# Expert rows loaded as 32 by 32 blocks and transposed by VectorE, in place of a TensorE transpose

## The chip, the cores and the metric

The kernel runs on one core of one Trainium2 chip. The metric is the device time of one execution in microseconds (us). The kernel before took 1431.74 us (median of 3 runs, 1426.88 to 1431.79).

## What is computed

Four blocks follow each other, each with a residual sum and a layer norm: an attention with 16 heads over 16 batches of 256 rows, a mixture of experts, a second attention with 16 heads of width 8, and a gated recurrence. The change touches the second block only. Cut to it:

```python
def _L0_ffn_ref(x, keys, w1, b1, w2, b2, rw, rb):      # E, TOP_K = 16, 4;  D = 128;  F = 512
    logits = -dist2 + jnp.einsum('bld,ed->ble', x, rw) + rb
    topv, topi = jax.lax.top_k(logits, TOP_K)
    w = jax.nn.softmax(topv, axis=-1)
    hidden = jax.nn.gelu(jnp.einsum('bld,efd->blef', x, w1) + b1, approximate=False)
    exp_out = jnp.einsum('blef,edf->bled', hidden, w2) + b2
    sel = jnp.take_along_axis(exp_out, topi[..., None], axis=2)
    return jnp.sum(w[..., None] * sel, axis=2)
```

Each of the 4096 rows goes to 4 of 16 experts.

## The kernel before, in words

**Stages.** The first stage computes the first attention and the router, and GpSimd scatters each row of 128 floats four times into the DRAM tensor `xs`, sorted by expert. The expert stage (about 689 to 977 us of the profiled span) then works through `xs` in NT = 144 tiles of GT = 128 rows. The second attention and the recurrence follow; their loops end the kernel. Every engine has a program of its own, written out by hand in this order, and semaphores join them.

**The expert stage, tile n.**
- SyncE (SP) reads the tile's row number out of the SBUF tensor `plan` (`row_of`, L416), loads the 128 rows (64 KB) from `xs` into `xg`, a ring of four buffers (`load_rows`, L423; the first four at L462), and later stores the tile's result from `yrow` into the same rows of `xs` (`store_rows`, L429). Its loop (L463 to L474) issues the load of tile n + 4, then the store of tile n - 4. It also carries the first transfers of the second attention (L439, L446, L454, L456) between tiles 95 and 102. SP executes in order: whatever it spends on one issue delays all that follow.
- TensorE (PE) transposes the rows with a multiplication by `ident` into a PSUM bank (`rows_in`, L899), two tiles ahead; it multiplies with the first weights (L911, four matmuls, each shown as two in the trace) and, for tile n - 2, with the second (L922, the same number).
- VectorE (DVE) copies the weights of tile n + 2 out of `wall` (L1473 and L1476), copies the transposed rows from PSUM to `xgT` (`rows_T`, L1480) and adds the bias to the result of tile n - 2 (L1502).
- ScalarE (ACT) applies the Gelu to the four hidden blocks (L1175).
- GpSimd (POOL) gathers finished rows for the second attention (L598), paced by the semaphore of `wA`.

`xg`'s buffer n % 4 is free for tile n + 4 when tile n has been transposed: `load_rows` waits for `tin_mm`, which PE raises.

The one place in which the order of SP's work is written:

```python
            for n in range(NT + 4):
                if n + 4 < NT:
                    load_rows(n + 4)
                if n >= 4:
                    store_rows(n - 4)
```

Of the kernel before, what the change touches and what calls it, by code (L numbers as in the profile page):

```python
# [12 lines left out]
B, N, D = 16, 256, 128  # L13
# [14 lines left out]
BIG = 1.0e30  # L28
EPS = 1e-5
GT = 128  # L30
CAP = TOK + GT
DUMMY = E * CAP
NT = (TOK * TOPK + E * (GT - 1)) // GT
NT += NT % 2
FULL = TOK * TOPK // GT
ROWS = DUMMY + (NT - FULL) * GT
LEVELS = TOK // GT
WA = F + FC
# [74 lines left out]
def build(nc, t, out):  # L113
    ctx = ExitStack()
    with ctx:
        def sb(name, shape, dt=fp32, c=ctx):
            return c.enter_context(nc.sbuf_tensor(name, shape, dt))

        def sem(name):
            return ctx.enter_context(nc.semaphore(name))  # L120

        psum = ctx.enter_context(nc.psum_tensor("psum", [128, 8 * 512], fp32))
        bank = [psum[:, i * 512:(i + 1) * 512] for i in range(8)]


        ident = sb("ident", [128, 128])
# [29 lines left out]
        a = ExitStack()  # L156
# [103 lines left out]
        xg = sb("xg", [128, 4, D], c=e2)  # L260
        xgT = sb("xgT", [128, 4, GT], c=e2)
        wA = sb("wA", [128, 4, WA], c=e2)
# [18 lines left out]
        tg = sb("tg", [128, N])  # L281


        TI, DN = [bank[3], bank[4]], [bank[5], bank[6]]
        S0, S1, PTA, PTB, OTB, J, Y, M = bank

        def up(n, f):

            return bank[(2 * n + f // 2) % 3][:, (f % 2) * GT:(f % 2 + 1) * GT]

        def rows_of(b):
# [3 lines left out]
        xs = nc.dram_tensor("xs", (ROWS, D), fp32, kind="Internal").ap()  # L295
# [6 lines left out]
            scores shifted_ready exps rinv_ready pn_ready pn1_ready pt_mm ptA_ev ptB_ev pv_mm ot_ev wo_mm res_ready bo_mm  # L302
            var_ready pow_ready x1c_ready m_x x1T_ready m_l mask_ready m_r pos_ready xsq_ready x1_kept scat exp_w top_ready
            ksq_ready rmat_ready b2_kept a_done plan_ready zrow_ready plan_out plan_in filled
            b2_mm xg_in0 xg_in1 xg_in2 xg_in3 tin_mm xgT_ready wA_ready wB_ready up_mm hid_ready dn_mm yrow_ready ys_out0 ys_out1
            cw_in lora_mm c_set cleared mrow_in to_full to_free st_full exps1 s_full max_done pv_full o_free full0 full1 free0 free1 a1_ready parts_ready
            qkd_out stk zeros_out nm_ready x2_ready x2_kept x3_ready x3_kept gate_act scan_done
            yk_in0 yk_in1 gates_in weighed comb_done var2_ready pow2_ready posc_ready xo_kept h_full fin_dve var3_ready pow3_ready scale_ready h_act fin_ready out_done""".split()
        s = {n: sem(n) for n in names}
# [11 lines left out]
        def need(eng, name, n):  # L321

            if not isinstance(n, int) or n > 0:
                eng.wait_ge(s[name], n)

        def need_alone(eng, name, n):


            if not isinstance(n, int) or n > 0:
                eng.wait_ge(s[name], n)  # L330
                eng.sem_inc(s["went_on"], 1)
# [42 lines left out]
        def _(sp):  # L374
# [17 lines left out]
            nothing = zrow[:, :].rearrange("q (o d) -> q o d", o=1).to_broadcast([128, E, D])  # L392
            for c in range(CAP // 128):
                if c % 2 == 0 and c > 0:
# [15 lines left out]
            sp.wait_ge(s["plan_in"], 16)  # L410
            sp.wait_ge(s["filled"], 16 * (CAP // 128 + 1))

            def row_of(n):
                at = 2 * n + 1
                src = plan[0:1, at:at + 1] if isinstance(n, int) else plan[0:1, bass.ds(at, 1)]
                return sp.value_load(src, min_val=0, max_val=ROWS - GT)  # L416

            row = {}

            def load_rows(n):  # L420
                need_alone(sp, "tin_mm", n - 3)
                row[n] = row_of(n)
                sp.dma_start(xg[:, n % 4, :], xs[bass.ds(row[n], GT), :]).then_inc(s[f"xg_in{n % 4}"], 16)  # L423

            def store_rows(n):

# [32 lines left out]
                row[n] = row_of(n)  # L459
            sp.wait_ge(s["scat"], 16 * B * TT * TOPK)  # L460
            for n in range(4):
                sp.dma_start(xg[:, n, :], xs[bass.ds(row[n], GT), :]).then_inc(s[f"xg_in{n}"], 16)  # L462
            for n in range(NT + 4):  # L463
                if n + 4 < NT:
                    load_rows(n + 4)
                if n >= 4:
                    store_rows(n - 4)
                if n == 95:
                    store_parts(-2)
                if n == 98:  # L470
                    sp.wait_ge(s["zeros_out"], 16)
                    sp.wait_ge(s["cleared"], 1)
                if n in (98, 100, 102):
                    load_stack(-2, 0, (n - 98) // 2)  # L474
# [24 lines left out]
        def _(pool):  # L499
# [4 lines left out]
            for it in range(TT):  # L504
# [8 lines left out]
                   allow_small_or_imprecise_dtypes=True).then_inc(s["cst"], 1)  # L513
            g.iota(first_row[:, :], pattern=[[CAP // 16, E]], base=0, channel_multiplier=0,
                   allow_small_or_imprecise_dtypes=True).then_inc(s["cst"], 1)
# [219 lines left out]
        def _(pe):  # L735
# [156 lines left out]
            pe.wait_ge(s["b2_kept"], E // 4)  # L892


            def rows_in(n, buf, loads):

                need(pe, f"xg_in{buf}", loads)
                need(pe, "xgT_ready", n - 1)
                nc.tensor.transpose(TI[buf % 2][:, 0:GT], xg[:, buf, :], ident[:, :]).then_inc(s["tin_mm"], 1)  # L899

            rows_in(0, 0, 16)
            pe.wait_ge(s["c_set"], 1)
            def tile(n):
                if n < NT:
                    need(pe, "xgT_ready", n + 1)
                    need(pe, "wA_ready", n + 1)
                    need(pe, "hid_ready", 4 * n - 4)
                    for f in range(FC):
                        if f == 2:
                            need(pe, "hid_ready", 4 * n - 2)  # L910
                        mm(up(n, f), wA[:, n % 4, f * 128:(f + 1) * 128], xgT[:, n % 4, :], start=True, stop=True).then_inc(s["up_mm"], 1)  # L911
                if n == 0:
                    rows_in(1, 1, 16)
                if n + 2 < NT:
                    rows_in(n + 2, (n + 2) % 4, 16 * ((n + 2) // 4 + 1))
                if 0 <= n - 2 < NT:
                    m = (n - 2) % 4
                    need(pe, "hid_ready", 4 * n - 4)
                    need(pe, "wB_ready", n - 1)
                    need(pe, "yrow_ready", n - 3)  # L920
                    for f in range(FC):
                        last = mm(DN[n % 2][:, 0:D], hid[:, m, f, :], wB[:, m, f * D:(f + 1) * D], start=(f == 0), stop=(f == FC - 1))  # L922
                    last.then_inc(s["dn_mm"], 1)
# [157 lines left out]
            for n in range(NT + 2):  # L1081
                tile(n)
                if n == 82:
                    attention(-3, -3 % 3, (7,))
                if n == 86:
                    attention(-2, -2 % 3, (1,))
                if n == 116:
                    attention(-2, -2 % 3, (7,))
# [190 lines left out]
        def _(dve):  # L1279
            v = nc.vector  # L1280
# [160 lines left out]
            v.tensor_scalar(used[:, :], tile_e[:, :], float(E), None, ALU.is_lt)  # L1441
            v.scalar_tensor_tensor(tile_r[:, :], tile_e[:, :], float(CAP), tile_r[:, :], ALU.mult, ALU.add)
            v.tensor_scalar(plan2[:, :, 0], tile_e[:, :], float(E - 1), None, ALU.min)
# [24 lines left out]
            def expert_of(n):  # L1468
                src = plan[0:1, 2 * n:2 * n + 1] if isinstance(n, int) else plan[0:1, bass.ds(2 * n, 1)]
                return dve.value_load(src, min_val=0, max_val=E - 1)  # L1470

            def weights_A(e, par):
                v.tensor_copy(wA[:, par, :], wall[:, bass.ds(e, 1), 0:WA].rearrange("q o c -> q (o c)")).then_inc(s["wA_ready"], 1)  # L1473

            def weights_B(e, par):
                v.tensor_copy(wB[:, par, :], wall[:, bass.ds(e, 1), WA:WCOLS].rearrange("q o c -> q (o c)")).then_inc(s["wB_ready"], 1)  # L1476

            def rows_T(n, buf):
                need(dve, "tin_mm", n + 1)
                v.tensor_copy(xgT[:, buf, :], TI[buf % 2][:, 0:GT]).then_inc(s["xgT_ready"], 1)  # L1480

            for n in range(2):
                first = expert_of(n)
                weights_A(first, n)
                weights_B(first, n)
            for n in range(2):
                rows_T(n, n)

            def tile(n):
                q = (n + 2) % 4  # L1490
                if n + 2 < NT:
                    e = expert_of(n + 2)
                    need(dve, "hid_ready", 4 * n - 4)
                    weights_A(e, q)
                    need(dve, "up_mm", 4 * n - 4)
                    rows_T(n + 2, q)
                if 0 <= n - 2 < NT:
                    m = (n - 2) % 4
                    need(dve, "dn_mm", n - 1)
                    if n >= 6:  # L1500
                        need(dve, f"ys_out{n % 2}", 16 * ((n - 6) // 2 + 1))
                    v.tensor_tensor(yrow[:, m, :], DN[n % 2][:, 0:D], wB[:, m, FC * D:FC * D + D], ALU.add).then_inc(s["yrow_ready"], 1)  # L1502
                if n + 2 < NT:
                    need(dve, "yrow_ready", n - 1)
                    weights_B(e, q)
# [204 lines left out]
```

## Time and profile before

| | |
|---|---|
| median of 3 runs | 1431.74 us |
| lowest and highest | 1426.88 and 1431.79 us |
| span of the profiled execution | 1445.1 us |
| mean granted TensorE clock over it | 0.960 of full speed |
| busy: PE, PE weight loads, DVE, ACT, POOL | 88%, 67%, 70%, 64%, 53% |

The profiled execution's record starts with its first and ends with its last instruction; no time around this span is listed for it, and the span is 13.4 us above the median of the runs. "Busy" counts instructions that compute. SP's instructions (register operations and the issue of transfers) are never counted as busy, so SP has no share on the page: its load is read from the timeline of its own queue, written SPq. A matmul here is a float32 one and appears as two instructions.

### The profile page before, as it was taken

The numbers are of one execution on the slowest core, as the hardware profiler recorded it, in microseconds if no ns is written. First come the engines' busy times: TensorE is split into PE (matmuls) and PEld (weight loads), VectorE is DVE, ScalarE is ACT, GpSimd is POOL, SyncE is SP. The second block draws the span as 40 slices with busy tenths as digits, with TensorE's granted clock in tenths as the row PEclk, the third lists the DMA queues.
The fourth block names the chain that finished last, engine by engine and source line by source line (L and its number), as shares of the span: only waits on it lengthen the run. The fifth ranks groups of instructions, "written<-read, shape, count | busy, mean of one in ns | idle before, by whom it ended". The sixth has DMA issues, their size and how long they took to land.

```text
span 1445.1 us, 36685 instructions
## 1 busy us (share of the span) xinstructions
PE 1272.4 (88%) x9756; PEld 971.6 (67%) x9756; DVE 1014.5 (70%) x3763; ACT 931.4 (64%) x2825; POOL 770.7 (53%) x981
## 2 busy tenths in 40 slices
PE   7999999999999999984899998996787788788973
PEld 3777776777777777764899998993455455455652
DVE  2677777777777777775677776766787677678835
ACT  5878777777777778772465665653565555556644
POOL 1557777777777777775222121235466666664132
PEclk9999999999999999997899999997899989999997
DMA  9612222221112222221222223222323223222102
GB/s 340 206 60 74 73 73 73 73 73 54 47 51 72 69 71 71 73 74 58 62 71 82 77 82 90 81 79 65 80 58 78 67 53 85 58 61 64 36 1 59
DMA packets 149016, 110.98 MB, mean 77 GB/s; under 512 B 12833, under 2 KB 137249, under 8 KB 148770
## 3 DMA queue, kind: packets, MB, share of 16 engines
q1 hardware_dynamic: 139842, 92.45, 22.0%
q0 software_dynamic: 8192, 16.79, 4.1%
q8 instruction: 46, 0.75, 0.2%
q14 instruction: 72, 0.59, 0.1%
q10 hardware_dynamic: 864, 0.39, 0.1%
HBM read 47.27 MB, written 61.93 MB: 76 GB/s over the span
## 4 chain that ended last, share of the span: by engine, by line
PE 60%; DVE 10%; issue 8%; ACT 7%; another core or an unknown queue 4%; DMA 3%; SPq 3%; DVEq 3%; ACTq 1%; POOL 0%; POOLq 0%
PE psum L911 9%; PE psum L922 8%; PE psum L798 6%; PE psum L835 6%; PE psum L853 5%; PE psum L746 4%; PE psum L815 3%; PE psum L753 3%; PE psum L947 3%; PE psum L747 3%; ACT wall L1183 2%; PE psum L935 2%; PE psum L1018 2%; ACT P L1153 2%
## 5 line engine op out<-in xcount | busy, mean ns | idle before, releaser
L554 POOL TENSOR_SCALAR P<-P,rinv 128x192 f32<-128x192 f32 (+1 forms) x384 | 308.5, 816 | 158.7 <-DVE rinv L1335 151.7
L1153 ACT ACTIVATE P<-shifted,least 128x192 f32<-128x192 f32 (+1 forms) x512 | 240.2, 470 | 100.6 <-DVE least L1321 99.1
L1175 ACT ACTIVATE hid<-psum,wA 128x128 f32<-128x128 f32 x576 | 164.4, 368 | 123.8 <-PE psum L911 120.2
L1512 DVE TENSOR_REDUCE mx<-psum 128x2 f32<-128x512 f32 x256 | 165.2, 687 | 66.4 <-PE psum L1018 42.3
L1321 DVE CUSTOM_DVE_ANT_0 shifted<-psum,band 128x192 f32<-128x192 f32 (+1 forms) x512 | 168.9, 385 | 27.5 <-PE psum L798 27.2
L598 POOL DMA_INDIRECT yk<-xs,posc x128 | 125.6, 981 | 107.4 <-DVE wA L1473 57.6
L1183 ACT ACTIVATE wall<-psum 128x1024 f32<-128x1024 f32 x128 | 130.8, 1022 | 65.7 <-PE psum L935 47.5
L911 PE MATMUL psum<-xgT,wA 128*128 128x128 f32 x1152 | 156.0, 279 | 2.0 <-ACT hid L1175 1.4
L922 PE MATMUL psum<-wB,hid 128*128 128x128 f32 x1152 | 152.6, 276 | 0.0
L911 PEld LDWEIGHTS psum<-xgT,wA 128*128 128x128 f32 x1152 | 143.3, 195 | 3.2 <-ACT hid L1175 1.8
L835 PEld LDWEIGHTS psum<-ident,P 128*128 128x128 f32 x1024 | 117.6, 141 | 35.8 <-issue 29.4
L544 POOL DMA_INDIRECT xs<-x1c,pos x120 | 120.3, 1002 | 39.1 <-issue 35.1
L922 PEld LDWEIGHTS psum<-wB,hid 128*128 128x128 f32 x1152 | 140.6, 193 | 0.0
L835 PE MATMUL psum<-ident,P 128*128 128x128 f32 x1024 | 134.9, 275 | 3.6 <-POOL P L554 1.5
L798 PE MATMUL psum<-kT,qT 64*128 64x192 f32 (+1 forms) x1024 | 131.5, 375 | 0.6 <-DVE least L1321 0.6
L853 PE MATMUL psum<-PT,V 128*64 128x256 f32 (+1 forms) x1024 | 111.0, 359 | 0.7 <-DVE PT L1309 0.7
L798 PEld LDWEIGHTS psum<-kT,qT 64*128 64x128 f32 x1024 | 80.2, 186 | 38.6 <-issue 36.9
L1153 ACT ACTIVATION_READ_ACCUMULATOR P<-shifted,least 128x1 f32 x512 | 95.9, 187 | 0.0
L1473 DVE COPY wA<-wall 128x516 f32 x144 | 63.0, 437 | 41.5 <-ACT hid L1175 28.0
L1309 DVE COPY PT<-psum 128x448 f32<-128x448 f32 x128 | 79.1, 618 | 16.9 <-PE psum L853 7.3
L746 PE MATMUL psum<-hT,wg 128*128 (+1 forms) x256 | 88.9, 429 | 1.4 <-ACT kT L1110 0.9
L1476 DVE COPY wB<-wall 128x640 f32 x144 | 74.2, 515 | 20.9 <-DVE yrow L1502 1.5
(261 smaller groups left out, 2537.0 us busy)
## 6 DMA issues: line engine op xcount, KB each, us to landing
xs<-zrow SPq DMA_DIRECT2D x34, 1024.0 KB
xg<-xs SPq DMA_DIRECT2D x144, 64.0 KB, 1.8
xs<-yrow SPq DMA_DIRECT2D x144, 64.0 KB
wall<-in_wall SPq DMA_DIRECT2D x1, 8232.0 KB, 36.3
qkd<-parts SPq DMA_DIRECT2D x64, 96.0 KB
kst<-qkd SPq DMA_DIRECT2D x22, 128.0 KB
qst<-qkd SPq DMA_DIRECT2D x22, 128.0 KB
wall<-qkd SPq DMA_DIRECT2D x20, 128.0 KB
```

The costliest lines, as they stand in the source:

```text
L554: g.tensor_scalar(x, x, rinv[:, par, n:n + 1], None, ALU.mult).then_inc(s["pn_ready"], 1)
L746: mm(J[:, 0:N], wg[:, r * 128:(r + 1) * 128], tok, start=True, stop=True)
L798: last = mm(bk[:, c0:c0 + w], qT[64 * h:64 * h + 64, p, it * 128:(it + 1) * 128], kT[64 * h:64 * h + 64, p, 0:w], start=True, stop=True)
L835: last = nc.tensor.transpose(bk[:, c0:c0 + 128], P[:, par1, it, h, jt * 128:(jt + 1) * 128], ident[:, :])
L853: last = mm(OTB[64 * h:64 * h + 64, k * N + c0:k * N + N], V[:, jt, r * 128 + 64 * h:r * 128 + 64 * h + 64], PT[:, k, h, keys], start=(jt ...
L911: mm(up(n, f), wA[:, n % 4, f * 128:(f + 1) * 128], xgT[:, n % 4, :], start=True, stop=True).then_inc(s["up_mm"], 1)
L922: last = mm(DN[n % 2][:, 0:D], hid[:, m, f, :], wB[:, m, f * D:(f + 1) * D], start=(f == 0), stop=(f == FC - 1))
L1153: last = sc.activation(P[:, par, it, h, 0:w], shifted[:, par, it, h, 0:w], ACT.Exp, scale=-1.0, bias=least[:, par, n:n + 1], accum_out=row ...
L1175: sc.activation(hid[:, n % 4, f, :], up(n, f), ACT.Gelu, bias=wA[:, n % 4, F + f:F + f + 1]).then_inc(s["hid_ready"], 1)
L1183: sc.activation(pc[:, p % 4, :, :, :].rearrange("q h j n -> q (h j n)"), ST, ACT.Exp, scale=SCALE1).then_inc(s["exps1"], 1)
L1321: v.tensor_tensor_reduce(out=shifted[:, par, it, h, 0:w], in0=bk[:, c0:c0 + w], in1=band[:, it, 0:w], scale=-SCALE0, scalar=3.0e38, op0=AL ...
L1512: v.tensor_reduce(out=mx[:, :, h], in_=SB[(par + 1 + h) % 3].rearrange("q (i n) -> q i n", i=TT), axis=mybir.AxisListType.X, op=ALU.max).t ...
```

## The change

Each tile's rows are loaded by four transfers in place of one. Transfer j takes the 32 columns 32j to 32j + 31 of all 128 rows and puts them on the partitions 32j to 32j + 31, so that each of its 128 pieces is 128 bytes long (before: 128 pieces of 512 bytes a tile; now 512 pieces of 128 bytes). In `xg` the 32 by 32 blocks then lie where the transposed tile wants them, and only the inside of each block is still to be transposed: VectorE does that in one instruction from `xg` to `xgT`. TensorE's transpose, its PSUM banks and the semaphore `tin_mm` go; SP waits for `xgT_ready` in its place, and VectorE waits for the transfers.

```diff
+BLK = 32
...
-        TI, DN = [bank[3], bank[4]], [bank[5], bank[6]]
+        DN = [bank[5], bank[6]]
...
+            def blocks_in(n):
+
+                src = xs[bass.ds(row[n], GT), :].rearrange("(i b) (j a) -> j b i a", b=BLK, a=BLK)
+                for j in range(D // BLK):
+                    dst = xg[BLK * j:BLK * (j + 1), n % 4, :].rearrange("b (i a) -> b i a", a=BLK)
+                    sp.dma_start(dst, src[j]).then_inc(s[f"xg_in{n % 4}"], 16)
+
             def load_rows(n):
-                need_alone(sp, "tin_mm", n - 3)
+                need_alone(sp, "xgT_ready", n - 3)
                 row[n] = row_of(n)
-                sp.dma_start(xg[:, n % 4, :], xs[bass.ds(row[n], GT), :]).then_inc(s[f"xg_in{n % 4}"], 16)
+                blocks_in(n)
...
             for n in range(4):
-                sp.dma_start(xg[:, n, :], xs[bass.ds(row[n], GT), :]).then_inc(s[f"xg_in{n}"], 16)
+                blocks_in(n)
...
-            def rows_in(n, buf, loads):
-
-                need(pe, f"xg_in{buf}", loads)
-                need(pe, "xgT_ready", n - 1)
-                nc.tensor.transpose(TI[buf % 2][:, 0:GT], xg[:, buf, :], ident[:, :]).then_inc(s["tin_mm"], 1)
-
-            rows_in(0, 0, 16)
...
-                if n == 0:
-                    rows_in(1, 1, 16)
-                if n + 2 < NT:
-                    rows_in(n + 2, (n + 2) % 4, 16 * ((n + 2) // 4 + 1))
...
             def rows_T(n, buf):
-                need(dve, "tin_mm", n + 1)
-                v.tensor_copy(xgT[:, buf, :], TI[buf % 2][:, 0:GT]).then_inc(s["xgT_ready"], 1)
+                need(dve, f"xg_in{buf}", 16 * (D // BLK) * (n // 4 + 1))
+                v.transpose(xgT[:, buf, :], xg[:, buf, :]).then_inc(s["xgT_ready"], 1)
...
+            dve.wait_ge(s["a_done"], 4)
             for n in range(2):
                 rows_T(n, n)
```

**On SP**, one turn of the loop in the middle of the expert stage. Before (ISA is register work: a row number or a transfer's address):

```order
L416 TENSOR_LOAD plan [waits tin_mm]
L416 ISA x2
L423 ISA
L423 DMA xg<-xs 128x128
L429 DMA xs<-yrow 128x128 [waits yrow_ready,ys_out0]
```

After the change:

```order
L417 TENSOR_LOAD plan [waits xgT_ready]
L417 ISA x2
L426 ISA
L426 DMA xg<-xs 32x4x32
L426 ISA
L426 DMA xg<-xs 32x4x32
L426 ISA
L426 DMA xg<-xs 32x4x32
L426 ISA
L426 DMA xg<-xs 32x4x32
L437 DMA xs<-yrow 128x128 [waits yrow_ready,ys_out1]
```

Three issues and three address computations are new, all of them ahead of the store. Of SP's rows in the whole program there are 878 before and 1742 after.

**On PE**, one turn of the expert stage, before:

```order
L899 MATMUL psum<-ident,xg 128x128 [waits xgT_ready,xg_in2]
L922 MATMUL psum<-wB,hid 128x128 [waits yrow_ready,wB_ready,hid_ready]
L922 MATMUL psum<-wB,hid 128x128 x3
L911 MATMUL psum<-xgT,wA 128x128 [waits hid_ready,wA_ready,xgT_ready]
L911 MATMUL psum<-xgT,wA 128x128
L911 MATMUL psum<-xgT,wA 128x128 [waits hid_ready]
L911 MATMUL psum<-xgT,wA 128x128
```

After the change:

```order
L919 MATMUL psum<-wB,hid 128x128 [waits yrow_ready,wB_ready,hid_ready]
L919 MATMUL psum<-wB,hid 128x128 x3
L912 MATMUL psum<-xgT,wA 128x128 [waits hid_ready,wA_ready,xgT_ready]
L912 MATMUL psum<-xgT,wA 128x128
L912 MATMUL psum<-xgT,wA 128x128 [waits hid_ready]
L912 MATMUL psum<-xgT,wA 128x128
```

Only the transpose is gone; PE no longer waits for a load itself.

**On DVE**, the same turn, before:

```order
L1473 COPY wA<-wall 128x516
L1480 COPY xgT<-psum 128x128 [waits tin_mm,up_mm]
L1502 TENSOR_TENSOR yrow<-psum,wB 128x128 [waits dn_mm]
L1476 ISA [waits yrow_ready]
L1476 COPY wB<-wall 128x640
```

After the change:

```order
L1470 COPY wA<-wall 128x516
L1477 STREAM_TRANSPOSE xgT<-xg 128x128 [waits xg_in2,up_mm]
L1500 TENSOR_TENSOR yrow<-psum,wB 128x128 [waits dn_mm]
L1473 ISA [waits yrow_ready]
L1473 COPY wB<-wall 128x640
```

The copy out of PSUM became the block transpose out of `xg`, in the same place, and the wait for the load moved to it.

## Rows read from the trace of the kernel before

**Rows 1.** The page, parts 1 and 2: busy time, granted clock and DMA by slices
```profile
PE 1272.4 (88%) x9756; PEld 971.6 (67%) x9756; DVE 1014.5 (70%) x3763; ACT 931.4 (64%) x2825; POOL 770.7 (53%) x981
...
PE   7999999999999999984899998996787788788973
...
PEclk9999999999999999997899999997899989999997
```
**Rows 2.** Timeline, all engines, one tile: start us, us, engine, line [idle before]
```profile
762.17 0.14 PEld L899 LDWEIGHTS psum<-ident,xg 128*128 128x128 f32 x1
762.28 0.27 PE L899 MATMUL psum<-ident,xg 128*128 128x128 f32 x1
762.39 1.06 PE L922 MATMUL psum<-wB,hid 128*128 128x128 f32 x8
...
763.15 0.28 DVE L1480 COPY xgT<-psum 128x128 f32<-128x128 f32 x1
...
763.28 1.06 PE L911 MATMUL psum<-xgT,wA 128*128 128x128 f32 x8
...
764.17 0.27 PE L899 MATMUL psum<-ident,xg 128*128 128x128 f32 x1
```
**Rows 3.** Timeline of SP's own queue between 755 and 764 us
```profile
756.64 0.34 SPq L423 DMA_DIRECT2D xg<-xs  x1
757.23 0.36 SPq L429 DMA_DIRECT2D xs<-yrow  x1
758.42 0.33 SPq L423 DMA_DIRECT2D xg<-xs  x1
...
760.19 0.33 SPq L423 DMA_DIRECT2D xg<-xs  x1
760.78 0.84 SPq L429 DMA_DIRECT2D xs<-yrow  x1
762.45 0.33 SPq L423 DMA_DIRECT2D xg<-xs  x1
```
**Rows 4.** Waits between 876 and 905 us; landing of the loads
```profile
PE psum L899 <- DMA xg<-xs: 5.7, 3, 2.2
...
DMA to landing us min/median/max: 1.6/1.8/3.2
```
**Rows 5.** Timeline of SP's queue: long issues, and other transfers between two loads
```profile
704.59 0.71 SPq L423 DMA_DIRECT2D xg<-xs  x1
...
851.02 1.06 SPq L429 DMA_DIRECT2D xs<-yrow  x1
...
874.20 0.35 SPq L429 DMA_DIRECT2D xs<-yrow  x1
874.66 3.45 SPq L439 DMA_DIRECT2D qkd<-parts  x4
879.05 0.34 SPq L423 DMA_DIRECT2D xg<-xs  x1
```
**Rows 6.** Timeline of SP's queue, the second and third of the first four loads
```profile
689.66 0.34 SPq L462 DMA_DIRECT2D xg<-xs  x1
690.18 0.33 SPq L462 DMA_DIRECT2D xg<-xs  x1
```
**Rows 7.** SP's instructions by line: duration ns min/median/max, first and last start us
```profile
L423 SPq DMA_DIRECT2D xg<-xs x140: 14/333/1181, 692.2 to 969.9; - x140
L439 SPq DMA_DIRECT2D qkd<-parts x64: 276/612/1493, 874.7 to 1344.2; - x64
L446 SPq DMA_DIRECT2D qst<-zeros x11: 244/252/606, 883.7 to 1346.6; - x11
```
**Rows 8.** Windows: us, PE, PEld, DVE, ACT, POOL busy (x), PEclk, DMA share, GB/s
```profile
692.00:696.00 4.00, 3.83 (x17) 3.43 (x18) 1.39 (x4) 1.49 (x5) 0.53 (x1) 0.50 0.08 22
...
740.00:760.00 20.00, 20.00 (x182) 20.00 (x181) 14.84 (x43) 11.88 (x42) 2.37 (x5) 1.00 0.26 72
...
890.00:900.00 10.00, 7.80 (x56) 7.62 (x54) 4.60 (x13) 3.62 (x13) 2.24 (x4) 0.83 0.32 94
```
**Rows 9.** DMA queues between 740 and 760 us: packets, MB, share of 16 engines
```profile
q1 hardware_dynamic: 3078, 1.41, 24.8%
```
**Rows 10.** Groups by line: count | busy us, mean ns | idle before
```profile
L1480 DVE COPY xgT<-psum 128x128 f32<-128x128 f32 x144 | 41.0, 285 | 12.2 <-PE psum L899 12.1
L1476 DVE COPY wB<-wall 128x640 f32 x144 | 74.2, 515 | 20.9 <-DVE yrow L1502 1.5
```

More of the change, by code:

```diff
@@ L304, in build @@
             ksq_ready rmat_ready b2_kept a_done plan_ready zrow_ready plan_out plan_in filled
-            b2_mm xg_in0 xg_in1 xg_in2 xg_in3 tin_mm xgT_ready wA_ready wB_ready up_mm hid_ready dn_mm yrow_ready ys_out0 ys_out1
+            b2_mm xg_in0 xg_in1 xg_in2 xg_in3 xgT_ready wA_ready wB_ready up_mm hid_ready dn_mm yrow_ready ys_out0 ys_out1
             cw_in lora_mm c_set cleared mrow_in to_full to_free st_full exps1 s_full max_done pv_full o_free full0 full1 free0 free1 a1_ready parts_ready
```

## The prediction
> **What bounds the kernel now.** I read the page first, then the timeline of one tile, then SP's own queue. The page [rows 1] says PE: 88% busy, more than any other engine, at nearly the full clock, and slices 20 to 27 (the expert stage) read 8 or 9 tenths. The change works inside that stage, so the question is what one tile costs there and on which engine. The timeline [rows 2] shows PE without a gap: transposes start at 762.28 and 764.17, so a tile takes 1.89 us, of which the sixteen matmul instructions take twice 0.89 (762.39 to 763.28 to 764.17) and the transpose 0.11 (762.28 to 762.39). The 0.27 us printed for the transpose is its length in the pipeline, not what it adds. DVE works 14.84 us of 20 and ACT 11.88 [rows 8]: both have room.
>
> SP does not appear in those shares, so its queue has to be read by starts [rows 3]. Loads are issued at 756.64, 758.42 and 760.19: one every 1.77 us. The tile on PE takes 1.89 us, so if SP were waiting for PE its loads would come every 1.89. They come faster because SP is catching up after a delay, such as the 0.84 us issue at 760.78, and while it does so 1.77 us is its own pace: row number, address, load, semaphores, store. **SP has only 0.12 us of room a tile.** A second sign: where SP puts four other transfers between two loads [rows 5], the distance from a store to the next load grows from the usual 1.19 us (757.23 to 758.42) to 4.85 us, and in this stretch PE stands waiting for `xg` three times, 5.7 us in all [rows 4], busy for only 7.80 of 10 us [rows 8]. So two engines run side by side at the same pace, and the one that has no share on the page is the one that the change loads.
>
> **The change part by part.**
> - *PE's transpose goes*: 0.11 us a tile, 144 tiles, 16 us. It is a gain only while PE sets the pace.
> - *DVE's copy becomes a block transpose*: the copy takes 0.285 us [rows 10]. A transpose is not in this trace. Below, it could be somewhat shorter than the copy; above, I bound it by the longest DVE instruction of the stage, 0.515 us for 640 columns. That is at most +0.23 us on an engine with 5.2 us free in 20, about 0.5 us a tile, so it is hidden and costed at nothing. Without that cover it would cost up to 33 us.
> - *The waits*: SP now waits for `xgT_ready`, raised by DVE after its transpose (its copy starts at 763.15, PE's transpose at 762.28 [rows 2]) in place of `tin_mm`, up to 1 us later; the buffer it frees is needed four turns later, and a load lands in 1.8 us [rows 4], so this costs nothing. On DVE a late load now holds up the bias addition and the copy of `wB` behind it, and with them SP's store; those too have four turns of SP before SP asks for them.
> - *Three more transfers a tile on SP*: this is the term that decides. The nearest row is the start of the stage, where loads with their row numbers already read are issued one after the other: starts at 689.66 and 690.18, 0.52 us apart, of which 0.34 is the issue and 0.18 the address [rows 6]. A block transfer has the same number of pieces (128) and its own address computation. Below: the shortest kind of issue in the trace, 0.25 us for a 24 KB transfer [rows 7], and 0.18 for the address, 0.43. Above: `qkd<-parts`, like the new ones a pattern with a middle dimension, 0.61 us [rows 7], and 0.18, 0.79. I take 0.52, because piece count, tensors and addressing are those of the row; the three-level pattern is what could move it up.
>
> **The sum.** SP's turn becomes 1.77 + 3 x 0.52 = 3.33 us, against 1.78 of PE work: SP alone sets the pace. Along its queue: the first 16 transfers take 8.3 us from 689.1, to 697.4. Then 140 turns of 3.33 are 466.2. The second attention's transfers, which stand between the turns, take 9.7 us more (3.7 of them in [rows 5], beyond the usual 1.19; the other three groups by the same subtraction). Now and then an issue is long, as at 760.78: between 700 and 860 us, 16 issues in 84 turns are over 0.5 us (the first and the last in [rows 5]), longer than usual by 8.7 us in all or 0.10 a turn. With nearly twice as many instructions in a turn I take 0.19, 27 us. The last load starts at 697.4 + 466.2 + 9.7 + 27 = 1200 us; it started at 969.9 [rows 7]. The difference is **+230 us**, and all later work waits behind it. Of the profiled span, 1445.1, that makes 1675; of the median of the runs, which lies 13.4 lower, **1662 us**. PE's 16 us are not subtracted: PE would be waiting in that time. For each 0.01 us that an issue differs from 0.52, the total moves by 576 x 0.01 = 5.8 us.
>
> A rule of the Trainium skill points the other way. In these rows, the issue of a load takes SP 0.52 us of a 1.77 us turn, and the issues bound it. "DMA: Bandwidth & Descriptors", section "Issuing engines are not separate DMA queues", says that the sequencer's time for starting a transfer is usually small relative to the transfer. By that rule four issues would vanish beside PE's work and the time would be that of the first rival; the trace agrees in that a transfer lasts longer (1.8 us) than its issue, but here the transfers overlap and the issues cannot.
>
> **The rivals.**
> 1. *PE still sets the pace, and the kernel is faster.* The place is SP's turn: if the four block issues took, with their addresses, no more than PE's tile leaves, the gain would be 144 x 0.11 = 16 us, 1416 us. A turn without its load issue is 1.77 - 0.52 = 1.25 us; four issues fit under the present average of 2.00 us a tile ((969.9 - 692.2) / 139, [rows 7]) only at 0.19 us each or less, and only then is the kernel not slower. Against it: the address alone takes 0.18, and no kind of issue in the rows is typically under 0.25 us. For it: only that a few single issues in [rows 7] are recorded far shorter than the median. 4 in 100, with 1 of these for a draw (within 0.5%, about what a measurement of this kernel can tell from no change).
> 2. *A block transfer costs much more than a plain load*, as `qkd<-parts` does: 0.79 us each, +230 + 576 x 0.27 = +386 us, 1817 us. The same end is reached if the DMA engines become the bound. Between 740 and 760 us, 3078 packets kept 16 engines busy for 24.8% [rows 9], 25.8 ns a packet. A tile has 288 packets with their 16-fold completions now and would have 720 (512 + 64 + 128 + 16). At the same price these are 1.16 us a tile; only at about four times that for each short one would they exceed SP's 3.33. For this rival: the pattern has three levels. Against: `qkd<-parts` has 192 pieces with a middle dimension of 3, not 128 with 4. 15 in 100.
> 3. *The clock.* After a pause the granted clock was 0.50 and eight matmul instructions took twice as long [rows 8]; sixteen then take 2 x 1.78 = 3.56 us, a little more than SP's turn. PE will be idle nearly half the time, so it may be granted the low level of its clock, 1.2 GHz, for stretches. If it stayed there, a tile would take 3.56 or somewhat more with the waits in it: 144 x up to 0.2 is +30 us on the forecast, 1692. It is inside the first case's range, and I give it no time of its own.
>
> The skill's page "DMA: Bandwidth & Descriptors", section "Specifications", states that below 512 B a transfer is done by read-modify-write. No row here shows pieces of 128 B by themselves; if such a piece cost twice 25.8 ns, the engines would need 2.0 us a tile, still under SP's turn, so the rule alone only supports the second rival's chance.
>
> **How the numbers follow.** SP's issues at about 0.52 us: 81 in 100, with 1610 us at 0.43 us an issue and 1740 with 0.60 us and the low clock. Rival 2: 15 in 100. Rival 1: 4 in 100. The range, 1600 to 1790 us, holds the first case with its bounds and the nearer part of rival 2 (an issue of up to 0.74 us). Faster 3 in 100, within 0.5% 1, slower 96.
>
> **What would show it.** In the profile of the changed kernel: block transfers 0.52 us apart in SP's queue, turns of 3.3 to 3.5 us with no waits of SP in them; DVE's transposes waiting for `xg` in nearly every tile; PE's matmuls of the expert stage idle before L912 on `xgT`; the stage 500 us long in place of 288, with the rest of the kernel unchanged; a lower clock and half the PE share in the stage. The prediction is wrong if turns stay below 2 us, if SP's queue shows waits for DVE, or if the loads land so late (well over 3 us) that DMA engines and not the issues set the pace.

## The result, and the profile after

The changed kernel takes 1640.5 us (median of 4 runs, 1636.9 to 1643.8) against 1429.3 before (4 runs, 1424.6 to 1431.8): ratio 1.150, 95% interval 1.147 to 1.153. It is **211 us slower**; the forecast was 1662, 230 slower. The profiled execution of the changed kernel took 1638.1 us, its span is 1636.2.

The page of the changed kernel, parts 1, 2 and 4 (spans; busy time; slices; chain):

```profile
span 1636.2 us, 37552 instructions
...
PE 1314.3 (80%) x9612; PEld 996.2 (61%) x9612; DVE 1035.6 (63%) x3763; ACT 932.2 (57%) x2825; POOL 770.5 (47%) x981
...
PE   7999999999999998476666666667667788788883
...
SPq 28%; DMA 10%; issue 9%; PE 6%; DVE 4%; ACT 1%; DVEq 1%; ACTq 0%
```

The same part 4 on the page of before:

```profile
PE 60%; DVE 10%; issue 8%; ACT 7%; another core or an unknown queue 4%; DMA 3%; SPq 3%; DVEq 3%; ACTq 1%; POOL 0%; POOLq 0%
```

Against [rows 1]: the slices of the expert stage, 8 or 9 tenths before, are mostly at 6 now. The chain of what ended last was PE for 60% of the span before; now SP's queue is its largest part with 28%, where it had 3% (the shares of the changed kernel add up to 59% of the span, the rest is not followed). The transposes are gone (144 matmul instructions fewer).

The timeline of SP's queue, which answers to [rows 3]:

```profile
800.93 1.81 SPq L426 DMA_DIRECT2D xg<-xs  x4
802.99 0.37 SPq L437 DMA_DIRECT2D xs<-yrow  x1
804.19 1.81 SPq L426 DMA_DIRECT2D xg<-xs  x4
806.25 0.37 SPq L437 DMA_DIRECT2D xs<-yrow  x1
807.45 1.81 SPq L426 DMA_DIRECT2D xg<-xs  x4
```

Four block transfers take 1.81 us from the start of the first to the end of the last, so with an issue of 0.317 they start (1.81 - 0.317) / 3 = 0.50 us apart. A turn is 3.26 us (800.93, 804.19, 807.45), which is 1.77 + 3 x 0.50. There is no gap in it that is larger than before: from the store to the next load it is 1.20 us, as it was 1.19. SP waits for nobody: the waits view of its queue between 691 and 1180 us has no entry (before, between 691 and 970 us: 8 waits, 3.8 us).

By line, the block loads (duration ns min/median/max, first and last start us) and the time to landing; VectorE's transpose; who waited for `xg`:

```profile
L426 SPq DMA_DIRECT2D xg<-xs x576: 316/317/1681, 688.7 to 1181.7; - x192
L1477 DVE STREAM_TRANSPOSE xgT<-xg x144: 304/311/313, 692.3 to 1183.5; 128x128 f32<-128x128 f32 x144
...
  DMA xg<-xs: 176.8, 137
...
DMA to landing us min/median/max: 1.5/1.7/3.2
```

From first to last load the stage takes 493.0 us (688.7 to 1181.7) where it took 689.1 to 969.9, 280.8: **+212 us, as much as the whole 211**. A second profile of the kernel before (e4 below) has 276 us there, and against it the stage is 217 us longer and the span 207. The 10 us between lie at its edges: the last load is followed by the last matmul of the first weights after 3.0 us (1181.7 to 1184.7) where it took 8.8 in e4, the rest of the kernel is 3 us shorter, and the first load starts 1.6 us earlier. A block transfer lands as fast as the plain load did (1.7 against 1.8 us, [rows 4]). VectorE waits 176.8 us for loads, in 137 of 144 tiles. Those are waits for loads that SP issued late.

TensorE behind it, in the timeline of all engines (idle time before an instruction in brackets):

```profile
801.29 2.07 PE L912 MATMUL psum<-xgT,wA 128*128 128x128 f32 x8 [0.63 <-DVE xgT L1477]
...
810.59 0.31 DVE L1477 STREAM_TRANSPOSE xgT<-xg 128x128 f32<-128x128 f32 x1 [1.05 <-DMA xg<-xs]
...
810.95 1.16 PE L912 MATMUL psum<-xgT,wA 128*128 128x128 f32 x8 [1.23 <-DVE xgT L1477]
...
700.00:900.00 200.00, 132.49 (x953) 120.77 (x952) 89.20 (x236) 70.39 (x247) 25.36 (x38) 0.94 0.20 42
```

The last line is the windows view of 200 us of the stage (columns as in [rows 8]): PE is busy for 66%, DVE for 45, ACT for 35, and the granted clock is 0.94. No compute engine is near its limit.

### The profile page after: what moved, and what is told of

Same layout as the page of the kernel before. It is cut to its first block, busy times and chain, and to the rows that moved or that the text cites. A ratio compares the mean times of both kernels' runs of the same rounds, so it can differ in the third digit from the quotient of the medians.

```text
span 1636.2 us, 37552 instructions
## 1 busy us (share of the span) xinstructions
PE 1314.3 (80%) x9612; PEld 996.2 (61%) x9612; DVE 1035.6 (63%) x3763; ACT 932.2 (57%) x2825; POOL 770.5 (47%) x981
## 4 chain that ended last, share of the span: by engine, by line
SPq 28%; DMA 10%; issue 9%; PE 6%; DVE 4%; ACT 1%; DVEq 1%; ACTq 0%
SPq L426 14%; DMA qst<-qkd 4%; SPq L437 4%; SPq L417 4%; DMA wall<-qkd 2%; SPq L462 2%; DMA qkd<-parts 2%; SPq L447 2%; SPq L464 1%; PE psum L1015 1%; PE psum L932 1%; DVE parts L1577 1%; DVE mx L1510 1%; PE psum L971 1%; ACT wall L1180 1%
## 5 line engine op out<-in xcount | busy, mean ns | idle before, releaser
L912 PE MATMUL psum<-xgT,wA 128*128 128x128 f32 x1152 | 185.9, 311 | 170.0 <-DVE xgT L1477 169.5
L912 PEld LDWEIGHTS psum<-xgT,wA 128*128 128x128 f32 x1152 | 158.8, 214 | 196.9 <-DVE xgT L1477 183.7
L919 PE MATMUL psum<-wB,hid 128*128 128x128 f32 x1152 | 169.4, 296 | 5.8 <-DVE yrow L1500 5.8
L919 PEld LDWEIGHTS psum<-wB,hid 128*128 128x128 f32 x1152 | 156.2, 211 | 6.8 <-ACT hid L1172 6.8
L1477 DVE STREAM_TRANSPOSE xgT<-xg 128x128 f32<-128x128 f32 x144 | 44.8, 311 | 177.3 <-DMA xg<-xs 176.8
L1015 PE MATMUL psum<-kst,qst 128*128 128x256 bf16 x352 | 60.2, 285 | 35.5 <-DMA qst<-qkd 23.0
```

## The experiments

The theory under test: **SP's turn, the sum of its issues and its register work, sets the pace of the expert stage.** Rivals: short pieces and the DMA engines; VectorE's transpose with its waits; the chain of latencies behind a late load. All times are medians; a ratio, with its 95% interval, is to fresh runs of the kernel before.

**e1: the issues alone.** TensorE's transpose and pieces of 512 bytes stay; only the load is cut in four by rows (the first four loads likewise, and PE waits for four times the count).

```diff
-                sp.dma_start(xg[:, n % 4, :], xs[bass.ds(row[n], GT), :]).then_inc(s[f"xg_in{n % 4}"], 16)
+                h = GT // PARTS
+                for j in range(PARTS):
+                    sp.dma_start(xg[h * j:h * (j + 1), n % 4, :], xs[bass.ds(row[n], GT), :][h * j:h * (j + 1), :]).then_inc(s[f"xg_in{n % 4}"], 16)
```

> The kernel before, TensorE's transpose kept, but each tile's rows loaded by four plain transfers of 32 rows (pieces of 512 bytes). Theory (SyncE's issues set the pace): the turn on SyncE's queue becomes 1.77 + 3 x 0.50 = 3.27 us as in the changed kernel, and the time is its time, 1429 + 211 = 1640 us (1615 to 1665). Rival (the 128-byte pieces and the DMA engines, or VectorE's transpose with its waits, cost the time): neither is here, so 1430 to 1460 us.

Measured: 1641.6 us (ratio 1.151, 1.148 to 1.155), within 1.1 us of the changed kernel. SP's queue in e1:

```profile
757.50 1.81 SPq L426 DMA_DIRECT2D xg<-xs  x4
759.55 0.37 SPq L437 DMA_DIRECT2D xs<-yrow  x1
760.75 1.81 SPq L426 DMA_DIRECT2D xg<-xs  x4
```

The same 1.81 and the same turn of 3.25 us, with TensorE's transpose in place and no short piece anywhere. This kernel reproduces the whole loss with nothing of the change but its number of issues and their addresses.

**e3: the pieces alone.** One transfer a tile, 512 pieces of 128 bytes. They repeat the first 32 columns of each row, so this kernel computes with the wrong columns; the amount of work is the same.

```diff
-                sp.dma_start(xg[:, n % 4, :], xs[bass.ds(row[n], GT), :]).then_inc(s[f"xg_in{n % 4}"], 16)
+                sp.dma_start(xg[:, n % 4, :].rearrange("q (j a) -> q j a", a=32), xs[bass.ds(row[n], GT), 0:32].rearrange("r (o a) -> r o a", o=1).to_broadcast([GT, 4, 32])).then_inc(s[f"xg_in{n % 4}"], 16)
```

> The kernel before with one transfer a tile, but made of 512 pieces of 128 bytes: it loads the first 32 columns of each row four times, so the experts work on repeated columns. Theory: one issue a turn, SyncE's turn stays near 1.77 us and the time near 1429 us (1420 to 1445). Rival (the short pieces make the DMA engines slow): 1470 us or more, with loads landing later than 2.5 us.

Measured: 1426.7 us against 1426.6, ratio 1.000 (0.998 to 1.002). The queue of e3 between 740 and 760 us (packets, MB, share of the 16 engines):

```profile
q1 hardware_dynamic: 7195, 1.42, 34.4%
```

In [rows 9] it was 3078 packets and 24.8%. The 4117 further packets cost the engines 9.6% of 16 x 20 us, 30.7 us, 7.5 ns each. The engines are a third busy, and the kernel's time does not move.

**e2 and e11: two transfers a tile**, cut by rows (64 partitions each) and by columns (128 partitions, 256-byte pieces). e2 is e1 with PARTS = 2; e11:

```diff
-                    sp.dma_start(xg[h * j:h * (j + 1), n % 4, :], xs[bass.ds(row[n], GT), :][h * j:h * (j + 1), :]).then_inc(s[f"xg_in{n % 4}"], 16)
+                    sp.dma_start(xg[:, n % 4, h * j:h * (j + 1)], xs[bass.ds(row[n], GT), h * j:h * (j + 1)]).then_inc(s[f"xg_in{n % 4}"], 16)
```

> The same with two transfers of 64 rows. Theory: turn 1.77 + 0.50 = 2.27 us. By the changed kernel's queue (16 first issues x 0.50, 140 turns x 3.26 and 27 us of other issues and long ones make its 493 us) the stage is 4 + 318 + 27 = 349 us from the first to the last load, against 281 before: +68 us, 1497 us (1480 to 1515). Rival (cost by bytes or pieces): 1430 to 1445 us.

Measured: 1536.2 us (ratio 1.076, 1.073 to 1.078), 39 more than expected and far from the rival's. The loads of e2 by line:

```profile
L426 SPq DMA_DIRECT2D xg<-xs x288: 468/492/814, 690.1 to 1079.3; - x144
```

An issue for 64 partitions takes 0.49 us, not 0.32. The turns that the timeline shows are 2.61 to 2.63 us (755.26, 757.87, 760.50; the next one, with a late store, 2.97), and the stage takes 389 us. So the theory held and the price I gave an issue was wrong. e11 was made to tell shape from number:

> As e2_split2, TensorE's transpose kept, two transfers a tile, but each over all 128 rows and half the columns (128 pieces of 256 bytes) in place of 64 rows. e2's issues took 0.49 us each. If that was the shape of 64 partitions, these take 0.33 as all with 128 do: turn 1.77 + 0.52 = 2.29 us, 1495 us (1480 to 1510). If it was the count of two or the size of 32 KB: again 0.49 and 1536 us.

Measured: 1492.7 us (ratio 1.045, 1.042 to 1.048). Its loads, by line and in the queue:

```profile
L426 SPq DMA_DIRECT2D xg<-xs x288: 332/333/1168, 693.1 to 1035.5; - x144
...
782.72 0.85 SPq L426 DMA_DIRECT2D xg<-xs  x2
...
785.00 0.85 SPq L426 DMA_DIRECT2D xg<-xs  x2
```

With 128 partitions it is 0.33 us an issue again, the turn is 2.28 us, and the time is 2 us from the expected one. So neither the count of two nor the size of 32 KB makes e2's issues slow; whether it is the 64 partitions or the 64 pieces, e2 cannot tell. One, two and four issues of about 0.32 us give 1427, 1493 and 1641 us. The first further issue costs 65 us and each of the next two 74. A room of 0.12 us in every turn would make this difference 140 x 0.12 = 17 us; it is 9, so less room than that was there on average.

**e5: one issue less for SP.** The changed kernel with the store on ScalarE's queue.

```diff
-                if n >= 4:
-                    store_rows(n - 4)
...
+                at = 2 * m + 1
+                r = act.value_load(plan[0:1, at:at + 1], min_val=0, max_val=ROWS - GT)
+                need_alone(act, "yrow_ready", m + 1)
+                need_alone(act, f"ys_out{m % 2}", 16 * (m // 2))
+                act.dma_start(xs[bass.ds(r, GT), :], yrow[:, m % 4, :]).then_inc(s[f"ys_out{m % 2}"], 16)
```

> The changed kernel with the store of each tile's result (and its own reading of the row number) moved from SyncE to ScalarE's queue; the four block loads stay. Theory (SyncE's turn alone sets the pace): a turn loses the 0.62 us from a store's end of the loads to the next row number (0.37 of issue and about 0.25 of waits), 3.26 to 2.64 us, 140 x 0.62 = 87 us less, 1640 - 87 = 1553 us (1535 to 1580). Rival (a load's landing and the chain VectorE, TensorE, ScalarE behind it, or the low TensorE clock, sets 3.3 us): 1620 to 1645 us.

Measured: 1555.2 us (ratio 1.088, 1.086 to 1.091), 85 less than the changed kernel and 2 from the expected time. Nothing was taken from the loads, the transposes or the compute engines; ScalarE even got more to do. Its loads by line:

```profile
L426 SPq DMA_DIRECT2D xg<-xs x576: 316/317/1941, 688.1 to 1094.8; - x192
```

The stage is 406.7 us long, 86 less than in the changed kernel.

**e6: shorter waits on SP.** The changed kernel with its three waits of a turn attached to the next instruction.

```diff
-                need_alone(sp, "xgT_ready", n - 3)
+                need(sp, "xgT_ready", n - 3)
...
-                need_alone(sp, "yrow_ready", n + 1)
-                need_alone(sp, f"ys_out{n % 2}", 16 * (n // 2))
+                need(sp, "yrow_ready", n + 1)
+                need(sp, f"ys_out{n % 2}", 16 * (n // 2))
```

> The changed kernel; SyncE's three waits of a turn no longer stand as instructions of their own with a counting increment behind each, but ride on the instruction that follows. Theory: each of the six small instructions gone is worth 0.02 to 0.05 us, the turn 3.26 to 3.0 to 3.15 us, so 1605 to 1625 us. Rival: no change, 1640 us, if something other than SyncE's turn sets the pace.

Measured: 1622.2 us (ratio 1.137, 1.133 to 1.141). In its queue the turns start at 786.03, 789.14 and 792.26, 3.11 us apart: 0.15 us less, times 140, is 21 us, and the time fell by 18. The loads of e6:

```profile
L426 SPq DMA_DIRECT2D xg<-xs x576: 316/317/1786, 688.2 to 1161.7; - x192
```

The stage is 473.5 us long, 19.5 less.

**e7 and e8: the block layout in one transfer**, and the same with e6's waits. This was the attempt at a kernel faster than both.

```diff
-                src = xs[bass.ds(row[n], GT), :].rearrange("(i b) (j a) -> j b i a", b=BLK, a=BLK)
-                for j in range(D // BLK):
-                    dst = xg[BLK * j:BLK * (j + 1), n % 4, :].rearrange("b (i a) -> b i a", a=BLK)
-                    sp.dma_start(dst, src[j]).then_inc(s[f"xg_in{n % 4}"], 16)
+                src = xs[bass.ds(row[n], GT), :].rearrange("(b i) (j a) -> j b i a", b=BLK, a=BLK)
+                dst = xg[:, n % 4, :].rearrange("q (i a) -> q i a", a=BLK)
+                sp.dma_start(dst, src).then_inc(s[f"xg_in{n % 4}"], 16)
...
-                v.transpose(xgT[:, buf, :], xg[:, buf, :]).then_inc(s["xgT_ready"], 1)
+                v.transpose(xgT[:, buf, :].rearrange("q (b i) -> q i b", b=BLK), xg[:, buf, :].rearrange("q (i a) -> q i a", a=BLK)).then_inc(s["xgT_ready"], 1)
```

> The changed kernel's block layout and VectorE's transpose, but in one transfer a tile: the rows of a block are taken 4 apart (row 4b + i in place of 32i + b), which makes the source a three-level pattern, and VectorE's transpose writes with a stride so that the order of rows is restored. Theory: one issue a turn, SyncE back at 1.77 to 1.82 us, TensorE at 1.78 without its transpose: 1429 - 16 = 1413 us at best, 1413 to 1430 with SyncE's long issues. Rival: a pattern whose outermost level is 4 may be spread over 4 DMA engines only; a tile is then 128 short pieces for each of them, by e3_pieces some 12 ns each, 1.5 us, beside the stores just under the turn, but if the pieces cost 25 ns they are 3.2 us a tile and the time is 1600 us or more. The strided transpose may also take VectorE longer than 0.31 us; up to about 0.8 it is hidden.

> e7 with the waits of e6. Theory: SyncE's turn falls below TensorE's 1.78 us, so TensorE's removed transposes come in full and part of the 6 us of starving goes: 1405 to 1415 us, 10 us or more below the kernel before. Rival (the load's landing or its DMA engines set the pace): the same as e7.

Measured: e7 1559.9 us (ratio 1.093, 1.091 to 1.095), e8 1551.6 (1.088, 1.085 to 1.090). e7 came out between its theory's time and its rival's. Its queue:

```profile
787.40 0.67 SPq L425 DMA_DIRECT2D xg<-xs  x1
788.34 0.81 SPq L436 DMA_DIRECT2D xs<-yrow  x1
790.18 0.66 SPq L425 DMA_DIRECT2D xg<-xs  x1
791.11 0.90 SPq L436 DMA_DIRECT2D xs<-yrow  x1
```

One issue of this pattern takes 0.66 us. The turn is 2.78 us (787.40 to 790.18), and VectorE waits for `xg` in 124 of 144 tiles. The bound is again in SP's queue, but two other instructions of SP have become longer with the load. By line, the store and the reading of the row number in e7 (duration ns min/median/max):

```profile
L436 SPq DMA_DIRECT2D xs<-yrow x144: 332/834/2617, 703.0 to 1108.2; - x144
L417 SPq TENSOR_LOAD <-plan x144: 261/444/707, 686.3 to 1097.3; - x144
```

In the changed kernel their medians are 374 and 266 ns. Against the 1.77 us of before, the load adds 0.32 us, the store 0.48 and the row number 0.18, together 2.75.

How the transfer is spread can be read from the packets of the whole program, on the pages of e3 and e7 in this order:

```profile
q1 hardware_dynamic: 195138, 92.45, 24.2%
...
q1 hardware_dynamic: 193410, 92.45, 22.2%
```

Both load 512 pieces of 128 bytes a tile. e7 has 1728 packets fewer, 12 a tile, and the packets missing are those of 4 bytes that report a completion: 4 a load where e3 has 16. That fits a transfer spread over 4 DMA engines and not 16, as the rival of the expectation had it; the packets carry no engine's number. In the traces of the two after 800 us the 512 pieces of a tile start within 1.35 to 1.53 us in e7 and within 0.57 to 0.79 in e3, except one of 1.23. That is still about half of a turn, so the engines do not set e7's pace. Why the store and the row number's reading get longer behind such a load stays open: the store issued at 802.44 us is done at 803.22, while the load's pieces start until 804.34, so it does not wait for them all.

e8's 0.15 us less register work brought 8 us in place of 20. Its store takes 957 ns at the median, 0.12 us more than e7's, and eats most of what was saved. (The waits view of e8 puts 39.5 us of the store on VectorE's bias addition; in tiles 60 to 62 that addition ended 8 us before the store of its tile, so this is no wait.)

**e9 and e10: the compute half of the change alone.** One plain load a tile, VectorE's transpose in place of TensorE's; e10 has e6's waits as well. Both leave the blocks where they lie, so the experts work on a scrambled tile of the same size.

```diff
-                src = xs[bass.ds(row[n], GT), :].rearrange("(i b) (j a) -> j b i a", b=BLK, a=BLK)
-                for j in range(D // BLK):
-                    dst = xg[BLK * j:BLK * (j + 1), n % 4, :].rearrange("b (i a) -> b i a", a=BLK)
-                    sp.dma_start(dst, src[j]).then_inc(s[f"xg_in{n % 4}"], 16)
+                sp.dma_start(xg[:, n % 4, :], xs[bass.ds(row[n], GT), :]).then_inc(s[f"xg_in{n % 4}"], 16)
```

> The change without its issues: VectorE's transpose in place of TensorE's, but the rows loaded by one plain transfer a tile. The blocks are then transposed where they lie and not exchanged, so the experts work on a scrambled tile. Theory: TensorE's tile falls from 1.89 to 1.78 us, but SyncE's turn is 1.77 and its long issues (0.10 a turn) now show: 2 + 140 x 1.77 + 27 = 277 us between first and last load against 281, so only about 4 of the 16 us come, 1424 us (1417 to 1430). Rival (SyncE is not bound at 1.77 us): the 16 us in full, 1412 us.

> e9 (scrambled tile as there) with the waits of e6, which took 0.15 us from SyncE's turn: 1.62 us, 0.16 below TensorE's tile. Theory: the 16 us come nearly in full, 1412 us (1407 to 1418). Rival: the same as e9.

Measured: e9 1421.3 us (ratio 0.996, 0.994 to 0.998), e10 1420.1 (0.995, 0.993 to 0.997). So taking the transpose off TensorE is worth 6 us in e9, of the 16 that a count of its instructions gives. This is e9's theory (1424 expected): SP holds the tile up. From the ninth load on, 98 of e9's 135 turns are 1.76 to 1.79 us long, SP's own pace, where the trace of before has 75. The windows view of e9 and e10 over the same stretch (PE is the first number after the length):

```profile
740.00:860.00 120.00, 118.73 (x1052) 117.85 (x1051) 90.66 (x273) 78.94 (x276) 23.01 (x32) 1.00 0.29 82
```
```profile
740.00:860.00 120.00, 119.53 (x1065) 119.06 (x1064) 91.41 (x277) 80.07 (x281) 22.18 (x31) 1.00 0.29 83
```

e10's PE has fewer gaps (0.47 us against 1.27) and its loads span 264 us (688.8 to 952.9) against 272 in e9, but the runs differ by 1 us, within their spread. The 1412 that I expected of e10 is 8 too low. SP did get its room: 48 of e10's 135 turns take 1.61 to 1.63 us. In its profiled execution the loads span 12 us less than in e4's, so in that one most of the 16 is there; why the median of the runs shows only 7 is not settled.

**e12 and e4: the kernel before**, with e6's waits, and with a blank line only.

> The kernel before with nothing but the waits of e6. Theory: SyncE's turn 1.62 us against 1.89 on TensorE, so SyncE catches up faster behind its other transfers and TensorE starves less: 2 to 8 us less than before, 1420 to 1426 us. Rival (no coupling): 1428 us.

> The kernel before with one blank line more: a second profile of it. The profiled execution of before was 1445.1 us long where its runs took 1425 to 1432. If its second attention (472 us from the end of the expert stage) was long by chance, this one is shorter by 10 to 20 us, span 1423 to 1435 us; if not, 1445 again. SyncE's turn is 1.77 us where it catches up, and the stage 281 us between first and last load, in both.

Measured: e12 1426.2 us (ratio 0.999, 0.998 to 1.001): no difference that can be told from none, as its rival had it, though the interval does not exclude the 2 or 3 us at the near end of the expectation. It is no version that beats the kernel before. In e4 one run took 1431.4 us with a span of 1429.6, so the 1445.1 us of the profiled execution of before were 15 us more than e4's. The part behind the expert stage shows where: from the last matmul of L911 (976.4 us) to the end it takes 469 us, in e4 454 (975.2 to 1429.6). The loads of e4 run from 690.3 to 966.4 us, 276 us; I had expected the same 281 as before. So single profiles of one kernel differ by 5 us in this stage, and differences of that size between the stages above mean nothing.

## Why the prediction was right

- **The bound.** It said that SP has 0.12 us of room a tile and no share on the page. e1, e5, e6 and e11 each moved SP's turn and nothing that another rival names, and the time followed at 140 turns. Confirmed. The room was even smaller than it said: with the 0.10 us of long issues that it counts itself, SP needs 1.87 of PE's 1.89 us on average. e9's gain of 6 us in place of 16 and e11's first step of 65 us (140 x 0.40 would be 56, 140 x 0.52 is 73) both show it.
- **The three issues a tile.** Taken as 0.52 us each from the first loads of the stage [rows 6]; measured 0.50. The turn was forecast at 3.33 us and is 3.26: 140 x 0.07 = 10 us of the 19 by which the forecast was high (in the time it is 21.5; the rest is the median of before, now 1429.3 and not 1431.7). This is the term that was mis-sized, by 4%.
- **The long issues.** 0.19 us a turn was a doubling of 0.10 because SP executes about twice the instructions. The stage leaves 493.0 - 16 x 0.50 - 140 x 3.26 = 28.6 us for them and the second attention's transfers; with 9.7 for the latter it is 0.13 a turn (0.15 when the first four turns, which have no store, are counted at the 2.64 us that they take). Counted as the prediction counted them, between 700 and 860 us, 6 issues are over 0.5 us and 5.0 us too long in all, about 0.10 a turn. So the doubling was wrong, 8 us of the 19. That the sum came within 19 us owes nothing to errors that cancel: both were too high.
- **PE's 16 us not subtracted.** Right; with SP at 3.26 us they are invisible.
- **VectorE's transpose at nothing.** It takes 0.311 us (copy: 0.285), between the bounds, and DVE is 45% busy. e1, without it, takes the same time.
- **Rival 1, PE sets the pace.** Excluded. It also sized PE's gain at 16 us; with SP's issues unchanged (e9) only 6 us are there, so with the old turn of SP the change had less to give than I wrote.
- **Rival 2, a dearer issue or the DMA engines.** Excluded for this change: a three-level pattern of 32 partitions costs no more than a plain load. But the spread I allowed for is real: 0.49 us for 64 partitions (e2) and 0.66 for e7's pattern. By `qkd<-parts`, 64 partitions as well, I had blamed the middle dimension; e2 has no such dimension and its issues are slower than those for 32 or 128 partitions too.
- **Rival 3, the clock.** The granted clock was 0.94 between 700 and 900 us, not half. PE worked at the low level in places (eight L912 instructions in 2.07 us at 801.29, in 1.16 at 810.95); the turn of SP around the slow ones is 3.26 us like the others (800.93 to 804.19), so it did not set the pace there.
- **The signs.** SP's turns (3.26 us, 3.46 on average with all that stands between them), VectorE's waits in nearly every tile, PE's idle time before L912 and the length of the stage (493 us for 500) came as named. PE's share did not fall to a half: it is 66%, and the granted clock stayed between 0.86 and 0.97 in stretches of 40 to 60 us from 700 to 1160 us.
- **Skill and rows.** The Trainium skill's "DMA: Bandwidth & Descriptors", "Issuing engines are not separate DMA queues", calls the sequencer's time for starting a transfer usually small relative to the transfer. For one load the traces do not go against it: 0.50 us to start, 1.7 to land. What the prediction drew from it, that the issues would vanish, is refuted: in e1 transfers of 16 KB overlap in flight and their issues do not, and in e5 the store's issue, taken off SP with its waits, is worth 85 us. The Trainium skill's "Specifications" on the same page has transfers under 512 bytes done by read-modify-write; whether these were, no run shows. In e3 the engines had 7.5 ns more to do per further packet, and the time did not move.

## What to carry to other kernels

An engine that only issues transfers can be the bound without any share on the page: read the spacing of its issues while it is catching up, and compare that with the period of the busiest engine. Before cutting a transfer into several, multiply the spacing of back-to-back issues (here 0.50 us with the address) by their number and set it against the room that this leaves. When work is taken off the busiest engine, look at the one that runs just beneath it: here 0.12 us a tile was the most that could be gained before SP took over, and its long issues used up most of that.

## What the runs showed of the hardware that was not expected

- An issue on SP's queue took 0.317 us for 32 partitions, 0.333 for 128 partitions with pieces of 512 or 256 bytes, 0.37 with 512 pieces of 128 bytes (e3), but 0.492 for 64 partitions (e2).
- e7's three-level load took 0.65 us to issue, ended in 4 completion packets where e3's ended in 16, and lengthened SP's instructions behind it: the store to 0.83 us at the median, from 0.37 in the changed kernel, and the reading of the row number to 0.44, from 0.27.
- VectorE's block transpose of 128 by 128 float32 numbers took 0.311 us, and 0.405 with an output written at a stride of four (e7).
- Three waits as instructions of their own, each with a counting increment, took 0.15 us of a turn (e6 against the changed kernel; the shortest turns of e9 and e10, 1.76 and 1.61 us, say the same).
- A packet of 128 bytes was cheap: 7.5 ns of one DMA engine for each further one (e3), where the average packet before cost 25.8 ns.
